# A gated two-expert MLP on rows sorted by expert, with both turns of a block ahead of the other block's gate-up steps

## The reference, cut to what matters

```python
vm = expert_mask(token_type_ids)[..., None]
...
mi = rms_norm(hidden_states, ln_post_attn_w)
v_out = jax.nn.silu(mi @ v_gate) * (mi @ v_up) @ v_down
l_out = jax.nn.silu(mi @ l_gate) * (mi @ l_up) @ l_down
hidden_states = hidden_states + jnp.where(vm, v_out, l_out)
```

## Time and profile before

| | |
|---|---|
| median of 3 runs | 1402.41 us (1401.85 to 1404.24) |
| the profiled execution, span | 1401.6 us, with a granted TensorE clock of 0.985 on average |
| PE busy | 1324.8 us (95%) |
| DVE, ACT, POOL busy | 869.6, 751.9, 436.4 us (62, 54, 31%) |
| phase 2, from the first gate product to the last addition | 470 to 672 us |

### The profile page before, as it was taken

One profiled execution on the slowest core, in us unless ns is written; L12 is line 12 of the kernel. 1 busy time (PEld: TensorE's weight loads), 2 busy tenths in 40 slices (PEclk: granted clock), 3 DMA queues, 4 the chain that ended last, 5 costly groups with the idle time before them and its releaser, 6 DMA issues.

```text
span 1401.6 us, 32322 instructions
## 1 busy us (share of the span) xinstructions
PE 1324.8 (95%) x10898; PEld 1102.3 (79%) x10898; DVE 869.6 (62%) x1837; ACT 751.9 (54%) x2859; POOL 436.4 (31%) x574
## 2 busy tenths in 40 slices
PE   7978999999997899999899999989989999998999
PEld 6844455555554799999888898889988888987999
DVE  4754566666667776557466666666666656556664
ACT  2323776657767622223866666663367666657422
POOL 1345666557665211000123332211013232323000
PEclk9989999999998999999999999999999999999999
DMA  5230000000000200000100000010001000000000
GB/s 180 79 116 20 5 5 5 0 4 4 4 0 1 98 2 0 0 0 1 65 5 6 4 4 4 1 72 28 0 1 65 6 4 4 7 0 1 9 22 30
DMA packets 13928, 30.33 MB, mean 22 GB/s; under 512 B 2832, under 2 KB 9488, under 8 KB 13200
## 3 DMA queue, kind: packets, MB, share of 16 engines
q1 hardware_dynamic: 13840, 29.23, 6.0%
HBM read 27.13 MB, written 2.10 MB: 21 GB/s over the span
## 4 chain that ended last, share of the span: by engine, by line
PE 73%; POOL 7%; DVE 7%; issue 7%; ACT 5%; POOLq 0%; DVEq 0%; ACTq 0%
PE bank L1029 64%; PE bank L1042 9%; POOL p L2015 2%; ACT p L1795 1%; POOL o L2015 1%; DVE stats L1457 1%; POOL xn L1980 1%; POOL kbd L1996 1%; DVE nmax L1532 1%; DVE pT L1427 1%; POOL kbd L2006 1%; POOL kbd L2015 1%; ACT kbd L1795 0%; DVE w_ff_rounded L1611 0%; POOL rstd L1962 0%
## 5 line engine op out<-in xcount | busy, mean ns | idle before, releaser
L1532 DVE TENSOR_REDUCE nmax<-bank 128x4 f32<-128x512 f32 x256 | 165.3, 684 | 96.0 <-PE bank L1029 94.6
L1029 PE MATMUL bank<-w_ff_rounded,hT_rounded 128*128 128x256 f32 x944 | 217.5, 285 | 4.2 <-ACT w_ff_rounded L1922 3.8
L1795 ACT ACTIVATE p<-bank,nmax 128x128 f32<-128x128 f32 x512 | 181.3, 397 | 70.1 <-DVE nmax L1532 70.0
L1427 DVE COPY pT<-bank 128x512 f32<-128x512 f32 x256 | 164.1, 680 | 88.0 <-PE bank L1042 87.7
L2015 POOL TENSOR_TENSOR p<-p,rshare 128x512 f32<-128x512 f32 x128 | 132.3, 1055 | 217.6 <-DVE rshare L1539 217.6
L1029 PE MATMUL bank<-xT_rounded,w_ff_rounded 128*128 128x256 f32 x864 | 196.3, 285 | 2.0 <-DVE x_all L1647 1.3
L1029 PE MATMUL bank<-xn_rounded,w_ff_rounded 128*128 128x256 f32 x608 | 172.0, 283 | 0.0
L1029 PE MATMUL bank<-xT_rounded,kbd_rounded 128*128 128x256 f32 x608 | 171.9, 283 | 0.0
L1029 PEld LDWEIGHTS bank<-w_ff_rounded,hT_rounded 128*128 128x128 f32 x944 | 163.7, 193 | 5.5 <-issue 4.2
L1029 PEld LDWEIGHTS bank<-xT_rounded,w_ff_rounded 128*128 128x128 f32 x864 | 148.7, 192 | 2.8 <-DVE x_all L1647 1.5
L1732 ACT ACTIVATE o<-bank 128x512 f32<-128x512 f32 (+1 forms) x104 | 60.4, 582 | 164.4 <-PE bank L1029 153.1
(11 more groups left out here) (182 smaller groups left out, 3126.9 us busy)
## 6 DMA issues: line engine op xcount, KB each, us to landing
ctxT<-in_ctxT SPq DMA_DIRECT2D x32, 128.0 KB, 2.4
w_ff<-in_w1b SPq DMA_DIRECT2D x6, 640.0 KB, 6.4
w_att<-in_w2a SPq DMA_DIRECT2D x1, 3072.0 KB
w_att<-in_w3a SPq DMA_DIRECT2D x1, 3072.0 KB
w_att<-in_w1a SPq DMA_DIRECT2D x1, 2304.0 KB
hT<-in_xT SPq DMA_DIRECT2D x8, 256.0 KB, 3.0
o<-in_x SPq DMA_DIRECT2D x8, 256.0 KB, 2.7
w_ff<-in_w2b SPq DMA_DIRECT2D x1, 2048.0 KB, 7.6
```

What stands on the lines that cost most here:

```text
L1029: return pe.matmul(dst, lhsT, rhs, start=first, stop=last)
L1427: dve.tensor_copy(dst, src).then_inc(sems[s[0], "copied"], 1)
L1532: dve.tensor_reduce(nmax[:, s[4], :], bank[:, :].rearrange("p (h t) -> p h t", h=QUAD), AX_X, ALU.max, negate=True).then_inc(sems[s[0], "m ...
L1795: t = act.activation(p[:, part], bank[:, part], ACT.Exp, bias=nmax[:, g, j:j + 1], accum_out=rsum[:, g, j:j + 1])
```

## The change

Phase 2 is written anew. Each token goes through its own expert alone. As phase 1 finishes a unit, POOL writes its 256 tokens with two indirect DMAs of 128 tokens each to a DRAM tensor `x_sorted`, at places that sort them by expert within each half of x (step `scatter`). The places come from `index_rows`, 28 small POOL instructions at POOL's entry of phase 1's loop, each waiting for the one before. Each half of 1024 tokens takes 9 blocks of 128 sorted tokens, because the two experts' parts both end inside a block; `x_sorted` is filled by four DMAs of POOL from DRAM to DRAM (16 x 9216 fp32 numbers each, 2.36 MB in all) when phase 0 begins, so that the places that no token takes hold numbers. The loop of phase 2 has 9 trips of two blocks instead of 4 trips of two units. SP loads a block, DVE and POOL normalise it, PE turns it (`xT1`), and the tokens are now stationary and the weights moving, gate and up together, in thirds of 2 x 230, 2 x 230 and 2 x 228 columns (`gu`, 6 matmuls each). Which expert's weights a block uses is an offset that PE reads from a table into a register ahead of `gu` and ahead of `down` (`value_load`, an instruction TENSOR_LOAD). The hidden row is turned (`hT`, 4 turns and 2 turns), `down` is 18 matmuls of 256 columns, ACT copies its result and SP stores it to `y_sorted`. Sixteen indirect DMAs of POOL (`gather`) add the results back into `x_all` at the boundary to phase 3: eight follow POOL's last step of phase 2 and eight stand among POOL's first `share` steps of phase 3.

```diff
 def steps_mlp1(norms, pre):
...
+    def part(u):
+        v, of_v = (B_, here) if u == A_ else (A_, ahead)
+        return (here(("hT", u, 0), ("hT", u, 1)) + of_v(("gu", v, 0)) + ahead(("norm_self", u)) + of_v(("gu", v, 1))
+                + ahead(("scale_mlp", u)) + of_v(("gu", v, 2)) + ahead(("xT1", u)) + here(("down", u)))
+
+    return part(A_) + part(B_)
...
-                ([], of_v(("cv", v), ("cq", v)) + keys_c[1:], here(("cdense", u, 1), ("end", u)))]
+                ([], of_v(("cv", v), ("cq", v)) + keys_c[1:], here(("cdense", u, 1), ("end", u), ("scatter", u)))]
...
+            def start_of(table, it, u):
+
+                return pe.value_load(table[0:1, bass.ds(it * UNITS + u, 1)], min_val=0, max_val=DC * GU)
...
+                    gu_of[u] = start_of(at_gu, it, u)
+                at, n = THIRDS[j]
+                for c in range(DC):
+                    x, x_lo = (rounded(x_part1(u, low)[:, c * P:(c + 1) * P]) for low in range(2))
+                    part = bass.ds(gu_of[u] + c * GU, GU)
+                    w, w_lo = (t[:, part].rearrange("p (g n) -> p g n", g=2)[:, :, at:at + n] for t in (w_high, w_low))
+                    mm(bank[:, 0:2 * n], x, w, c == 0, False)
+                    mm(bank[:, 0:2 * n], x_lo, w, False, False)
+                    t = mm(bank[:, 0:2 * n], x, w_lo, False, c == DC - 1)
...
+                start = start_of(at_down, it, u)
...
+            def scatter(ph, it, s, bank):
...
+                    pool.tensor_copy(dest_here[:, u, :], dest[:, rows(it, u)])
+                    pool.tensor_copy(staged[u], x_all[:, rows(it, u), :]).then_inc(staged_done, 1)
...
+                for b in range(ROWS):
+                    pool.indirect_dma_start(x_sorted, bass.IndirectOffsetOnAxis(to[b], 0), x_of[b], None)\
+                        .then_inc(scattered[u], 16)
...
+            def gather(ph, it, s, bank):
...
+                pool.indirect_dma_start(x_all[:, row_at, :], None, y_sorted[h],
+                                        bass.IndirectOffsetOnAxis(dest_in_half[:, row_at:row_at + 1], 0), compute_op=ALU.add)\
+                    .then_inc(y_added[h], 16)
```

More of the change, by code:

```diff
@@ L378 @@
     "nT2": "mm wide hi lo", "round": "done", "split": "lo", "finish": "hi", "cq": "mm copied", "ck": "mm flat",
[3 rows of a table removed]
+    "cv": "mm copied", "coT": "copied", "cdense": "mm", "xT1": "mm hi lo", "gu": "mm silu product", "hT": "mm hi lo",
+    "scatter": "", "mrow": "done", "ctx2": "near lo hi", "half": "done", "nT2_low": "",
+    "down": "mm copied", "q2": "mm copied", "k2": "mm copied", "v2": "mm copied", "oT2": "mm hi lo", "oT2_low": "",
     "wo": "mm", "w1": "mm gelu hi lo", "w2": "mm", "end": "done",
@@ L395, in __init__ @@
         self.index = index
+        self.iters = MLP_ITERS if index == 2 else ITERS
         self.layer, self.weave, norm, pre = PLAN[index]
@@ L425, in __init__ @@
                      for late, kind in enumerate(kinds) if 0 <= i - late < len(self.once)]
+        if index == 3:
+            self.once += [("gather", b) for b in range(B)]
         jobs = [s for s, _ in body if "mm" in EVENTS[s[0]]]
@@ L1003, in _ @@
                 if ph.index in (3, 5):
                     reader = lambda u: ("v2", u, ROWS - 1, 1)
-                    for u in range(UNITS):
-                        before, last = (PHASES[1], ("cv", u)) if ph.index == 3 else (PHASES[3], reader(u))
-                        sp.wait_ge(*after(before, ITERS - 1, last, "mm"))
-                        load_ctx(ph, 0, u, reader(u))
-                    ended(PHASES[ph.index - 1])
+                    if ph.index == 3:
+                        sp.wait_ge(*after(PHASES[2], MLP_ITERS - 1, ("down", B_), "mm"))
+                    else:
+                        for u in range(UNITS):
+                            sp.wait_ge(*after(PHASES[3], ITERS - 1, reader(u), "mm"))
+                            load_ctx(ph, 0, u, reader(u))
+                        ended(PHASES[ph.index - 1])
@@ L1261, in down, with turn_hidden @@
+            def turn_hidden(ph, it, s, bank):
+                u, j = s[1:]
+                pe.wait_ge(*after(ph, it, ("gu", u, 2), "product"))
+                starts = [f * P for f in range(QUAD)] if j == 0 else [QUAD * P, TAIL_FROM]
+                turn(s, ph.bank[s], [hidden[u][:, at:at + P] for at in starts])
             def down(ph, it, s, bank):
                 u = s[1]
-                pe.wait_ge(*after(ph, it, ("up1", u, 1, PRODUCTS), "h"))
-                pe.wait_ge(*split(ph, "experts", 17))
@@ new lines, in gu, with turn_hidden @@
+            def gu(ph, it, s, bank):
+                u, j = s[1:]
+                at, n = THIRDS[j]
+                act.wait_ge(*after(ph, it, ("hT", u, 1), "mm", back=1))
+                copy(ph, it, s, hidden[u][:, at:at + n], bank[:, 0:n], event="silu", func=ACT.Silu)
+            def turn_hidden(ph, it, s, bank):
+                u, j = s[1:]
+                part, n = (slice(0, QUAD * P), QUAD * P) if j == 0 else (slice(QUAD * P, F1C * P), (F1C - QUAD) * P)
+                act.wait_ge(*after(ph, it, ("down", u), "mm", back=1))
+                copy(ph, it, s, rounded(h_part1(u, 0)[:, part]), bank[:, 0:n], event="hi")
@@ L1867, in q2, with down @@
+            def down(ph, it, s, bank):
+                u = s[1]
+                act.wait_ge(y_out[u], 16 * (it + 1))
+                copy(ph, it, s, y_block[u], bank[:, 0:D])
             def q2(ph, it, s, bank):
@@ L1903, in round_piece @@
                     if s[1] != "kv":
[L1904 removed]
+                        act.wait_ge(*after(PHASES[2], MLP_ITERS - 1, ("gu", B_, 2) if s[1] == "q" and s[2] < 2 else ("down", B_), "mm"))
                 elif ph.index == 5 and s[1] == "o" or ph.index in (4, 6) and s[2] >= 4:
@@ L1914, in ctx2 @@
                 act.wait_ge(*after(ph, it, ("v2", u, ROWS - 1, 1), "mm", back=1))
+                if ph.index == 3 and isinstance(it, int) and it == 0:
+                    act.wait_ge(*after(PHASES[2], MLP_ITERS - 1, ("gu", B_, 2) if u == A_ else ("down", B_), "mm"))
                 act.activation(rounded(ctx_low(u)), ctxT[u][:, :], ACT.Copy).then_inc(sems[s[0], "near"], 1)
@@ L2030, in _ @@
                     pool.sem_inc(sems[kind, event], n)
+            for u in range(UNITS):
+                pool.sem_inc(y_out[u], 16)
             pool.sem_inc(primed, 1)
```

616 lines of the change are left out of this document (329 added, 287 removed), and 3 rows, old and new, of the table EVENTS.

## The result

The changed kernel took a median of 1465.88 us (1460.82 to 1468.24, four runs) against 1402.6 us (1401.85 to 1404.24, four runs): a ratio of 1.0444, with an interval of 1.0423 to 1.0465. It is slower, and by far more than the prediction's range allowed (1380 to 1433 us). The profiled execution is the shortest of the four, with a span of 1458.8 us; it is 57.2 us longer than the span of before.

A forecast was written before the change was run, and what follows sets the result against it. It took phase 2 as bound by PE's own work, with PE waiting for POOL at `scale_self`. Terms 1 + 7.6 + 18 + 0 - 26.4 + 5 = +5.2 on 1401.6, median 0.8 above: 1408 us, range 1380 to 1433.

The forecast's parts named there:

- six scatters at 3.0 us: Phase 1, POOL: five scatters straight ahead of `scale_self`, one ahead of shares PE awaits; 3.0 us each, +18 us.
- boundary 3: Boundary to phase 3: the second eight gathers stand ahead of and between POOL's first shares, half covered; +5 us (2 to 12).
- the index: Phase 1, ahead of the loop's first `scale_self`: 28 dependent POOL instructions 0.27 us apart, +7.6 us.
- The clock was a rival: Phase 2 slots: granted clock falls to 0.83, each slot's PE work 1.4 us longer, 25 us, 1433 us; chance 0.12.
- A slot: Phase 2, one block: 6.93 us of PE work, 1.2 waiting for scaling, two register loads at 0.64; 9.4 us.
- The wait for the scaling: Phase 2, every slot: the next block's scaling chain takes 3.65 us, PE covers 2.46 and waits 1.2 us.
- a load: Phase 2, two register loads per slot: 0.8 us each, about 0.16 covered by the running matmul, 0.64 exposed.
- Phase 2 as a whole: Phase 2's length: 175.5 us against 201.9 before, -26.4 us.
- The beginning: Start of phase 2: first block's gate-up 5.5 us, then a first slot of 16.0 us waiting for ACT's rounding.
- The tail: End of phase 2: last turns, loads, gate-up and `down`, with 1.4 us for ACT and DVE; 13.0 us.
- Phase 0: DRAM-to-DRAM fill of 2.36 MB beside the first loads, most of what it delays needed later; +1 us (0 to 6).
- My list of signs of being wrong: Slots under 8.7 or over 10.5 us, a scatter holding PE under 2 us, or PE waiting for anything else in a slot.

The follow-up runs named there:

- the last order: All moves together, with the next phase's weights rounded between the last block's thirds and the second block's part earlier, against the same without this order: 1357.54 us.
- the window above: Window over some ten phase 2 slots of the changed kernel with the next block's norm a third earlier; that kernel measured 1419.23 us.

## Why the prediction was wrong

**The step that failed** is this sentence: "what is put on POOL ahead of `scale_self` delays PE by its whole length". It is true of a pause of 1.34 us and false of one of 4.9. I read the place rightly and the bound rightly, but priced a pause by its length, and so six scatters at 3.0 us became +18. Measured, the five units with them grew by 7.0 us each, +35, and the sixth scatter with its boundary by 9.6 (forecast 3.0 and 0), of which 8.2 are slower work. These two rows hold 26.6 of the 52 us by which the sum was short; boundary 3 holds 12.1, phase 2 9.0, phase 0 3.5 and the index 0.8. Of the 4 us more for one scatter about 1 is a mis-sized term (3.9 to 4.1 us of POOL instead of 3.0: the wait for the copy's end and the gap between the DMAs) and about 3 are the half clock.

**The clock was a rival**, but in the wrong place. I gave it 0.12 for the slots of phase 2, and argued against it that "pauses in a slot are near 1 us, as in the loop of phase 1", while the same text forecast a pause of 3 us in that loop. The row with 0.62 was a warning for it: in the kernel before it is the start of ten microseconds at 0.50 behind a pause of PE of 2.56 us (ending at 445.84). In the slots it did come, in five of 15, behind two pauses of 0.84 and 0.72 us close to one another. The Trainium skill, TensorE: Matmul & The Clock Gate, section A second HAM failure mode: psum-queue depth-cycling, tells of a kernel whose short idle moments between groups of products let the clock swing between its two levels; the slots here are such a case, at 0.53 in one stretch and 1.00 in the next.

**A slot: right by two errors.** 9.4 forecast, 9.67 measured. The wait for the scaling is 0.84 to 0.88 us (1.2 forecast); a load, of a number that lies on the chip, takes 0.30 us (0.8 taken, from a transfer out of DRAM), yet costs PE 0.6 to 0.8 ahead of `down` (0.64 forecast), because it starts only when the turn does, and 0.3 or nothing ahead of gate-up (0.64 forecast). The half clock, 1.4 us in five slots of 15, fills part of what these leave. That the mean came out near the forecast is luck. That a load's number "is used by the very next matmul, so PE can't go on without it" left out that the sequencer reaches it ahead of the array.

**Phase 2 as a whole**: -17.4 for -26.4, 9 us short. The 15 slots are 4 us over (145.0 for 141). The beginning is near the forecast: 18.8 us to the turn in the first slot and some 3.2 for its load and `down`, against 5.5 + 16.0. In part this too is luck: the wait of 7.35 us in it is not ACT's rounding alone, for ACT's last rounding ends at 539.2 and DVE then still waits 2.42 us for the block, whose load the forecast put at nothing ("they cost nothing"), and half clock follows. The tail is 4.4 us over (17.4 for 13.0, from the end of the last slot's `down` at 694.4): the sum allowed 1.4 us for ACT and DVE there, PE waits 4.83 at 706.65, and products 0.21 us apart follow.

**Boundary 3**: +17.1 for a term of +5 with 12 as its upper bound. I asked only what the gathers do to POOL's shares. One of the four waits there came through DVE, which needs `x_all` and waits for the gathers' landing (5.11 us on PE), and the other three stay when those gathers are moved. Each has half clock behind it.

**Phase 0**: +4.5 for +1, inside the bounds given (0 to 6), but only by luck. The collision with the first loads made the first `scale_self` 7.6 us late (76.17 before, 83.79 after). Some 3 of these came back ahead of the loop, where the kernel before ran at half clock three times (14 us in all) and the changed kernel once (3.4 us), behind pauses of the same length. **The index**: +8.4 for +7.6, right for the pause: 28 dependent instructions of POOL in 8.3 us, 0.30 each. The half clock behind it, some 3 us more, was left out there too.

My list of signs of being wrong hardly shows it: slots between 8.7 and 10.5, a scatter over 2 us, no other wait inside a slot but the first. It watched the length of single steps; the clock stands beside it for the slots only.

What stays open: why five slots of the 15 fall to half clock and the others don't, with nearly the same pauses (0.86 and 0.71 us in a slot of 8.9; all five are among the seven slots in which the pause ahead of `down` is 0.71 us or more); what starts and keeps the half clock from 505 to 526; and what makes the pause of 3.95 us at 738, which every version has kept. The order of the rounding has a part in those at 706 and 717: the last order shortened them by 1.9 and 2.0 us, but the time did not show it.

## What to carry to other kernels

Price a pause of the matrix engine by its length only where it is short beside what the trace shows it to bear without losing its clock; here 1.0 us of added work cost 1.0 where the pause came to 1.3 to 1.7 us and the clock held, 2.5 and 4.1 where it fell, and 4.5 us cost 7.3. When a step must be added to an engine that the matrix engine waits for, look first for a place just behind what it waits for instead of ahead of it: the same two DMAs cost 7 us ahead of it and at most 0.6 behind it. And a new chain of small steps (statistics, factor, scaling) wants to start one stage earlier than its own length suggests, since a wait also uncovers whatever the sequencer would have hidden behind it.

## What the runs showed of the hardware that I had not expected

- In phase 1 the granted clock fell to 0.50 for 6 to 14 us behind every pause of 4.2 to 5.4 us, with and without DMAs, and stayed at 1.00 behind single pauses of 0.7 to 1.4 us. Behind pauses of 1.6 to 2.4 us it fell in some places and not in others, and so it did behind 0.84 and 0.72 us close together.
- A register load takes 0.30 us, and nothing of it shows where the sequencer is ahead of the array: in the 72 us of the window above, some ten slots with two loads each, PE was idle for 0.09 us.
- An indirect DMA of 128 rows of 1 KB holds POOL for 1.03 us when it scatters and 1.57 us when it gathers with an addition, with 0.30 us to the next; a scatter lands after 2.5 us, a gather after 3.8.
- POOL waits 0.81 to 0.91 us from the end of its own copy until it issues a DMA that reads it.
- A block's load of 128 KB lands after 2.1 us in the median, but after 10.1 and 10.5 us when it is issued right behind a load of 3 MB.
